# Moving the four decay exponentials of a chunked RWKV-6 recurrence ahead of the subtile loop, eight cores of one Trainium2 chip

## What is computed

```
wv = tanh((x + delta*w_mu) @ w_w1.T) @ w_w2.T + w_b2
w  = -exp(wv)                      # per head, 128 channels
# chunk of 32 tokens, wc = cumsum(w) inside the chunk
kw = k * exp(wc[-1] - wc);  qe = q * exp(wc - w);  ke = k * exp(-wc)
S  = S * exp(wc[-1]) + kw.T @ v    # state, chunk after chunk
o  = qe @ S + tril(qe @ ke.T, -1) @ v + diag(q*u*k) @ v
s  = (groupnorm(o) * silu(g)) @ o_w.T
out = x + s * silu(ffn(x))
```

## Time and profile before

| | us |
|---|---|
| median of the timed runs (2) | 4530.27 |
| lowest, highest | 4528.23, 4532.31 |
| the profiled execution | 4427.46 |
| its span on the slowest core (core 2) | 4425.9 |
| spans of the eight cores | 4391.1 to 4425.9 |

### The profile page before, as it was taken

The page is one execution under the profiler, slowest core; times in us unless marked ns, Lnnn a source line. Parts: engine busy times, 40 slices in busy tenths (PEclk is TensorE's granted clock), DMA queues, the critical chain, the costliest instruction groups (busy, mean ns, idle before and its releaser), DMA issues.

```text
span 4425.9 us, 36031 instructions; the slowest of 8 cores (4391.1 to 4425.9 us)
## 1 busy us (share of the span) xinstructions
PE 2181.7 (49%) x11424; PEld 968.6 (22%) x11424; DVE 1449.0 (33%) x2844; ACT 1423.8 (32%) x1552; POOL 300.3 (7%) x525
## 2 busy tenths in 40 slices
PE   0387324862257632675317752187432873238722
PEld 0132111321123211232102321032211322113211
DVE  0230452314432154321533225331343314533044
ACT  0342423424233332432323333243322423334241
POOL 1010000100011000110001000010000100001000
PEclk9998567985678856887558875598666986669856
DMA  9545004450235302453024420254203541034500
GB/s 157 104 81 89 11 12 84 78 88 5 36 74 91 62 5 53 71 84 55 10 52 76 81 48 10 57 86 74 41 10 67 91 73 30 11 72 81 95 5 15
DMA packets 88440, 257.76 MB, mean 58 GB/s; under 512 B 10206, under 2 KB 10527, under 8 KB 84639
## 3 DMA queue, kind: packets, MB, share of 16 engines
q0 software_dynamic: 83088, 221.82, 29.8%
q1 hardware_dynamic: 5168, 33.62, 3.4%
HBM read 443.65 MB, written 33.55 MB: 108 GB/s over the span
## 4 chain that ended last, share of the span: by engine, by line
DVE 20%; PEldq 19%; issue 17%; DMA 14%; ACT 11%; PEld 8%; ACTq 5%; another core or an unknown queue 3%; DVEq 2%; POOL 1%; POOLq 0%; SPq 0%
PEldq L285 18%; ACT L146 10%; DMA sb_fu<-w_fu 7%; ACTq L151 5%; DVE sb_qg L146 4%; DMA sb_x<-x 4%; DVE sb_z L146 3%; DMA sb_vgo<-w_g 3%; DVE sb_gst L146 2%; DVE sb_S L146 2%; DVE sb_o L146 2%; DVE sb_xin L146 1%; DVEq L144 1%; PEld Po L741 1%
## 5 line engine op out<-in xcount | busy, mean ns | idle before, releaser
L146 ACT ACT_TABLE_LOAD x704 | 903.2, 1283 | 2966.4 <-PEq L285 2040.4
L1156 PE MATMUL PtrT<-sb_id,sb_z 128*128 128x128 bf16 x256 | 32.4, 306 | 659.7 <-DVEq L151 659.7
L407 PE MATMUL PtrT<-sb_id,sb_xnt 128*128 128x128 bf16 x256 | 32.4, 306 | 506.9 <-DVEq L151 370.0
L146 DVE COPY sb_gff<-PtrT 128x512 bf16<-128x512 bf16 x64 | 27.2, 425 | 737.8 <-PEq L285 737.8
L577 PE MATMUL Pa<-sb_xnT,sb_fg 128*128 128x512 bf16 x768 | 190.6, 393 | 69.4 <-DMA sb_fu<-w_fu 34.5
L577 PE MATMUL Psm<-sb_xnT,sb_fg 128*128 128x512 bf16 x768 | 182.2, 380 | 60.7 <-DMA sb_fu<-w_fu 39.3
L557 POOL DMA_DIRECT2D sb_fg<-w_fg x192 | 108.7, 566 | 1425.4 <-PEq L285 1386.1
L146 DVE SCALAR_TENSOR_TENSOR sb_hall<-Pb,sb_scr 128x512 bf16<-128x512 f32 x96 | 66.4, 692 | 423.2 <-ACTq L151 417.9
L146 DVE TENSOR_SCALAR sb_qg<-sb_qe,sb_G 128x32 bf16<-128x32 bf16 x768 | 179.9, 234 | 75.0 <-ACTq L151 10.6
L459 PE MATMUL Pb<-sb_hall,sb_fd 128*128 128x512 bf16 x768 | 200.4, 425 | 7.5 <-issue 7.5
L459 PE MATMUL Pa<-sb_hall,sb_fd 128*128 128x512 bf16 x768 | 195.8, 418 | 7.4 <-issue 7.4
(11 more groups left out here) (174 smaller groups left out, 3464.4 us busy)
## 6 DMA issues: line engine op xcount, KB each, us to landing
sb_fg<-w_fg POOLq DMA_DIRECT2D x192, 256.0 KB, 4.0
sb_fu<-w_fu POOLq DMA_DIRECT2D x192, 256.0 KB, 4.8
sb_fd<-w_fd POOLq DMA_DIRECT2D x64, 768.0 KB, 7.9
sb_x<-x SPq DMA_DIRECT2D x32, 512.0 KB, 3.5
sb_vgo<-w_v POOLq DMA_DIRECT2D x8, 2048.0 KB, 18.6
sb_vgo<-w_g POOLq DMA_DIRECT2D x8, 2048.0 KB, 15.7
sb_vgo<-w_o POOLq DMA_DIRECT2D x8, 2048.0 KB, 17.4
out<-sb_sg POOLq DMA_DIRECT2D x32, 512.0 KB, 5.4
```

The source lines that it names most:

```text
L146: return fn(*a, **k)
L407: e.transpose(Ptr[:, c * 128:(c + 1) * 128], sb_xnt[:, 0, c * 128:(c + 1) * 128], sb_id[:])
L1156: e.transpose(Ptr[:, c * 128:(c + 1) * 128], sb_z[:, c * 128:(c + 1) * 128], sb_id[:])
```

## The change

The four `rA` steps of a megatile are taken out of the subtile loop and written one after the other between `ppd_t` and the first `rB1`. The matmuls go to Pa and Pb in turn, the Exps to `sb_scr` and `sb_z` in turn (both read as float32), and the eight split results have places of their own in the half of `sb_xin` that is free in this stage. The waits are those of two buffers: a matmul from the third on waits for the Exp two before it, and an Exp for the split two before it. The matmuls of `rB1` and `pg_t` read the new places and wait for the last of the four splits (`wspall`). Nothing else is changed; the numbers of matmuls, Exps, splits and blocks stay.

```diff
-        rA(it, s, m, 0)
+        for wts in range(NST):
+            bank = Pa if wts % 2 == 0 else Pb
+            def pw2_t(e, en, wts=wts, bank=bank):
...
+                    en.w(cs, ev[f"wexp{wts-2}"])
+                e.matmul(bank[:, 0:512], sb_h1[:, wts * 128:(wts + 1) * 128],
+                         sb_ww2[:, :], start=True, stop=True)
...
+            def pw2_s(e, en, wts=wts, bank=bank):
+                en.w(ct, ev[f"w2t{wts}"])
+                if wts == 0:
+                    en.w(ct, ev[f"gft{NC-1}"])
+                elif wts == 1:
+                    en.w(ct, st.get("z_rd_t", 0))
+                else:
+                    en.w(cv, ev[f"wsp{wts-2}"])
+                wf = wf_ap if wts % 2 == 0 else wf2_ap
+                e.activation(out=wf, in_=bank[:, 0:512], func=AF.Exp)
...
+                e.tensor_copy(out=whi4[wts], in_=wf)
+                e.tensor_tensor(out=wlo4[wts], in0=wf, in1=whi4[wts],
+                                op=ALU.subtract)
...
+        ev["wspall"] = ev[f"wsp{NST-1}"]
         for ts_ in range(NST):
             rC1(it, ts_)
-            if ts_ + 1 < NST:
-                rA(it, s, m, ts_ + 1)
             rC2(it, ts_)
...
             def parg_t(e, en, ai=ai, msk=msk, bank=bank, ts_=ts_):
-                en.w(cv, ev[f"wsp{ts_}"])
+                en.w(cv, ev["wspall"])
```

More of the change, by code:

```diff
@@ L821, in emit_megatile, with pw2_v, pwhid @@
         on("tensor", ppd_t)
-        rA(it, s, m, 0)
+        wf2_ap = sb_z[:].bitcast(F32)
+        whi4 = [sb_xin[:, 1, w, :] for w in range(NST)]
+        wlo4 = [sb_xin[:, 1, NST + w, :] for w in range(NST)]
+        st["whi4"] = whi4
+        st["wlo4"] = wlo4
+        for wts in range(NST):
+            bank = Pa if wts % 2 == 0 else Pb
+            def pw2_t(e, en, wts=wts, bank=bank):
+                en.w(cs, ev["h1"])
+                if wts == 0:
+                    en.w(cs, st["pa_free_s"])
+                elif wts == 1:
+                    en.w(cs, st["pb_free_s"])
+                else:
+                    en.w(cs, ev[f"wexp{wts-2}"])
+                e.matmul(bank[:, 0:512], sb_h1[:, wts * 128:(wts + 1) * 128],
+                         sb_ww2[:, :], start=True, stop=True)
+                ev[f"w2t{wts}"] = sig_t(e)
+            on("tensor", pw2_t)
+            def pw2_s(e, en, wts=wts, bank=bank):
+                en.w(ct, ev[f"w2t{wts}"])
+                if wts == 0:
+                    en.w(ct, ev[f"gft{NC-1}"])
+                elif wts == 1:
+                    en.w(ct, st.get("z_rd_t", 0))
+                else:
+                    en.w(cv, ev[f"wsp{wts-2}"])
+                wf = wf_ap if wts % 2 == 0 else wf2_ap
+                e.activation(out=wf, in_=bank[:, 0:512], func=AF.Exp)
+                ev[f"wexp{wts}"] = sig(e, cs)
+            on("scalar", pw2_s)
+            def pw2_v(e, en, wts=wts):
+                en.w(cs, ev[f"wexp{wts}"])
+                if wts == 0:
+                    en.w(ct, projev[3])
+                wf = wf_ap if wts % 2 == 0 else wf2_ap
+                e.tensor_copy(out=whi4[wts], in_=wf)
+                e.tensor_tensor(out=wlo4[wts], in0=wf, in1=whi4[wts],
+                                op=ALU.subtract)
+                ev[f"wsp{wts}"] = sig(e, cv)
+            on("vector", pw2_v)
+        ev["wspall"] = ev[f"wsp{NST-1}"]
+        st["argA_free"] = ev["wexp2"]
+        st["argB_free"] = ev["wexp3"]
+        if f"whi_{it}" in dumps:
+            def pwhid(e, en):
+                en.w(cv, ev["wsp0"])
+                e.tensor_copy(out=sb_whi[:].rearrange("p h t -> p (h t)"),
+                              in_=whi4[0])
+                ev["whid"] = sig(e, cv)
+            on("vector", pwhid)
+            dump(f"whi_{it}", sb_whi, cv, ev["whid"])
         rB1(it, 0)
@@ L849, in emit_megatile @@
         st["vgo_rd"] = ev["sprj3"]
[L851 to L885, removed]
     def rB1(it, ts_):
@@ L899, in parg_t @@
                     en.w(cs, st["argA_free"])
-                    en.w(cs, st["pa_free_s"])
                 if ai == 1:
                     en.w(cs, st["argB_free"])
+                whi = st["whi4"][ts_]
+                wlo = st["wlo4"][ts_]
                 for h in range(NH):
-                    e.matmul(bank[:, h * 128:(h + 1) * 128], sb_whi[:, h, :],
+                    e.matmul(bank[:, h * 128:(h + 1) * 128],
+                             whi[:, h * 128:(h + 1) * 128],
                              msk[:], start=True, stop=False)
-                    e.matmul(bank[:, h * 128:(h + 1) * 128], sb_wlo[:, h, :],
+                    e.matmul(bank[:, h * 128:(h + 1) * 128],
+                             wlo[:, h * 128:(h + 1) * 128],
                              msk[:], start=False, stop=True)
@@ L944, in pg_t @@
                 en.w(cs, ev[f"gs{ts_-1}"])
+            whi = st["whi4"][ts_]
+            wlo = st["wlo4"][ts_]
             for h in range(NH):
-                e.matmul(Psm[:, h * 8:(h + 1) * 8], sb_whi[:, h, :], sb_pm[:],
+                e.matmul(Psm[:, h * 8:(h + 1) * 8],
+                         whi[:, h * 128:(h + 1) * 128], sb_pm[:],
                          start=True, stop=False)
-                e.matmul(Psm[:, h * 8:(h + 1) * 8], sb_wlo[:, h, :], sb_pm[:],
+                e.matmul(Psm[:, h * 8:(h + 1) * 8],
+                         wlo[:, h * 128:(h + 1) * 128], sb_pm[:],
                          start=False, stop=True)
```

## The result

| | us |
|---|---|
| changed kernel, median of 16 executions | 4480.15 (4462.42 to 4536.72) |
| kernel before, median of 15 executions | 4456.38 (4419.39 to 4644.24) |
| ratio | **1.0079, 95% interval 1.0052 to 1.0107** |
| profiled execution of the changed kernel | 4470.26 |
| its spans by core | 4438.7 to 4468.7 |

The change costs 0.8%. The ratio and its interval leave out disturbed executions, among them the two of the kernel before that were timed ahead of the change (4528 and 4532 us, over 2% above the best of the fifteen); in later executions of this kernel that took 4534 and 4543 us, the four cores of one die had a granted clock of 0.72 to 0.73 and the others 0.75 to 0.76.

The account below looks back on a forecast made before the run. No engine is full; a chain of waits bounds the kernel. 4427.46 + 49.5 - 4.7 = 4472.3 us profiled (+1.01%), carried to the median as 4530.27 x 1.0101 = 4576 us; range 4540 to 4610.

Parts of the forecast that it names:

- 4530.27 x 1.0101 = 4576 us: Last step: carries the profiled execution's predicted +1.01% over to the timed runs' median of 4530.27 us.
- Three more steps at the start: Start of each recurrence: three more bare table loads and Exps on ACT, 6.19 us in each of 8 megatiles, +49.5 us.
- Three steps less at the boundaries: Subtile boundaries: `pov_v` no longer waits for DVE's split, gaining 0.43 us at 11 of 24 boundaries, -4.7 us.
- Earlier masked matmuls: After a boundary: the next subtile's first two Exps start sooner, worth nothing since the third needs a buffer freed after `pov_v`.
- The chain as drawn: Rival, boundaries: 3.8 us of decay step bought back 24 times, net -42 us, 4487 us as a median; chance 4%.
- One table load for a row of Exps: Rival, start: only the first of four decay Exps loads a table, saving 30.7 us, 4545 us as a median; 4%.
- Steps without overlap: Rival, start: each Exp waits for the split before it, 80.4 us for three rounds, 4608 us as a median; 4%.
- PE's clock: Rival, boundaries: PE's clock stays at 0.50, up to 72.7 us more, 4650 us as a median; slower by over 2%, 5%.

Follow-up runs that it names:

- e2: Changed kernel with the four decay steps ahead of the loop done twice; ratio to the kernel before 1.0256.
- e5: Changed kernel with decay matmuls and Exps ahead of the bonus' matmuls, DVE alternating one split with a quarter of the bonus scalings; ratio to the kernel before 1.0000.
- e6: Kernel before with only the first decay step, and the first two groups of masked matmuls with their Exps, moved ahead of the bonus' matmuls; ratio 0.9925.
- e1: Kernel before without the three decay steps inside the subtile loop, the decay of subtile 0 used for all four; ratio 1.0008.
- e4: Changed kernel with its four decay matmuls in one block, four Exps in one block and four float32 buffers; no usable ratio, profiled execution 4477.33 us.
- e7: Kernel before with the same instructions, waits and order, written as one block per engine; ratio 0.9086.
- e10: e1 with the loop's three decay matmuls left in; no ratio given, recurrence 211.2 us, PE's output and state at the second boundary 2.42 us.
- e11: The very kernel of e1 profiled once more; recurrence 211.1 us, PE's output and state at the second boundary 2.30 us.
- e3: Changed kernel with masked matmuls and the chunk decays' matmul waiting for their own subtile's split, not the last of four; ratio to the kernel before 1.0098.

## Why the prediction was right or wrong

*The time was wrong, and the step that failed is the last one:* "4530.27 x 1.0101 = 4576 us". On its own base the sum was right: 4472.3 us for the profiled execution, which took 4470.26; and a ratio of 1.0101 against a measured 1.0079 with 1.0052 to 1.0107. That the two single executions agree within 2 us is partly luck: timed executions of the changed kernel spread by 30 us and more. What was wrong is the base. I had written that no view explained the 2.3% between the median of two runs and the profiled execution, and yet carried the sum over to it. The fifteen executions of the kernel before show a median of 4456 us, 74 us lower, and nearer to the profiled one; with it the same ratio gives 4501 us. The range, 4540 to 4610, was built around that one base and had no room for another; the measured 4480 lies 60 us below it. A difference of 100 us without a cause should have been an end of the range, from 4472 up.

*Three more steps at the start, +49.5 us:* right. The blocks follow at 2.03, 2.09 and 2.09 us, and the start grew by 6.28 us, 50.2 in all. e2 gives the same price per step, e5 and e6 show that it is paid because nothing covers it.

*Three steps less at the boundaries, -4.7 us:* right in mechanism and nearly in size. The gaps behind PE's end shrank by 0.12, 0.25 and 0.35 us, 5.8 us in eight megatiles, and the boundaries by 0.84 us, 6.7 in all. Over the eight cores of the kernel before, `pov_v` came late (0.55 us or more behind PE's end) at 92 of 192 boundaries, 11.5 a core; I had reckoned 11. The 0.05 us of the first boundary that I left out were 0.12, and the gap there is now 0.13 us, not the 0.2 to 0.25 that I had said for every boundary. e1 shows the limit of this term: where PE's clock fell otherwise, the gaps shrank by 0.76 us and only 0.2 of it arrived.

*Earlier masked matmuls, worth nothing:* right in the main. The changed kernel's masked matmuls start 0.23 us behind PE's output stage, yet the time from `pov_v` to the first factor fell by only 0.09, 0.04 and 0.00 us at the three boundaries, 1 us in eight megatiles. The gaps (0.72 us less) and PE's stage (some 0.16 more) leave 0.3 us of the 0.84 over: this 0.1, and 0.2 ahead of the product with `sb_gff`, whose cause no run shows.

*The chain as drawn:* refuted by e1. *One table load for a row of Exps:* 704 loads, refuted as a result of this change; e4 and e7 show the load to go with the block. *Steps without overlap:* refuted by e2. *PE's clock:* not as a loss of 73 us, but the clock does decide between 1.47 and 2.72 us at the second boundary, and these 1.25 us are more than the whole gain of the three boundaries.

## What to carry to other kernels

A step that runs in the shadow of another engine's work costs its own time again when it is grouped with its like and moved to a place where nothing else runs. Before such a move, look at what runs beside the step now and what will; the chain of waits shows only the last to arrive. And a base time that the profile does not bear out belongs in the range, not in the middle of it.

## What the runs showed of the hardware

- A table load of 1283 ns comes with the block of ACT, not only with a change of function: 704 loads here, 57 with one block per engine (e7), 680 when four Exps share a block (e4). In the one block of e7, Exps and the Square behind them follow without a load, the Sqrt has one (at 478.22 us on core 5), and the Exp behind it has one again (at 502.25).
- One block per engine took 9.1% off the kernel (e7). This is the loads and the branches together; no run separates them.
- PE's output and state stage takes 1.47 us at a granted clock of 1.00 and 2.72 us at 0.50. In the kernel before, over eight cores and eight megatiles, the first boundary had the lower clock in all 64 cases, the third in 1, the second in 23. At the second the mean was 2.3 to 2.4 us in three runs without the loop's decay (e1, e10, e11) and in e3, 1.9 before, 2.1 in the changed kernel, 1.6 in e2 and 1.5 in e5. e1 and e11, the same kernel, had the lower clock in 45 and 46 of the 64 cases: repeatable for that kernel, cause open.
